# The last stage of a four-stage network on one core: bias by a one-row matmul, scale and shift on ScalarE, the row added behind, stores on SyncE

## The reference, cut to what matters

```python
for e in range(4):
    sl = slice(e * n, (e + 1) * n)
    m = d // 2 ** e
    out = attn_out[:, sl, :m] @ o_w[:m, :m].T + o_b[:m]
    outs.append(pad(out, d - m) + xn[:, sl, :])      # xn = layernorm of x
x = x + _layernorm(concatenate(outs))                # no weight, no bias, eps 1e-5
```

## Time and profile before

| | us |
|---|---|
| median of 3 runs | 5076.88 (5074.21 to 5078.27) |
| the profiled execution's own time | 5076.77 |
| its span | 5074.3 |
| last stage, first `AT` load issued to the end of the span | 4967.76 to 5074.3 |

### The profile page before, as it was taken

One profiled execution on the slowest core, in us unless ns is written; L12 is line 12 of the kernel. 1 busy time (PEld: TensorE's weight loads), 2 busy tenths in 40 slices (PEclk: granted clock), 3 DMA queues, 4 the chain that ended last, 5 costly groups with the idle time before them and its releaser, 6 DMA issues. The chain is left out here.

```text
span 5074.3 us, 90035 instructions
## 1 busy us (share of the span) xinstructions
PE 4656.5 (92%) x33915; PEld 2063.8 (41%) x33915; DVE 4191.1 (83%) x5487; ACT 3425.1 (67%) x6144; POOL 1333.4 (26%) x881
## 2 busy tenths in 40 slices
PE   6998776896999999999999999999998889999993
PEld 3333542562333333333333333333334445555532
DVE  6999640796999999999999999999993877777736
ACT  4878110232888888888888888888885426666663
POOL 2333210462000000000000000000001229999992
PEclk9999887995999999999999999999997769999996
DMA  5111569686333333333333333333313831322305
GB/s 183 58 54 42 187 241 390 201 271 136 49 49 49 49 49 52 53 53 53 49 49 49 49 49 49 54 54 54 49 20 125 297 101 43 82 61 73 79 5 169
DMA packets 383090, 479.51 MB, mean 94 GB/s; under 512 B 164544, under 2 KB 277984, under 8 KB 365760
## 3 DMA queue, kind: packets, MB, share of 16 engines
q1 hardware_dynamic: 369376, 455.41, 38.5%
q10 hardware_dynamic: 13280, 18.35, 1.1%
HBM read 315.71 MB, written 155.58 MB: 93 GB/s over the span
## 5 line engine op out<-in xcount | busy, mean ns | idle before, releaser
L792 DVE TENSOR_REDUCE at_NM<-at_MX 128x1 f32<-128x1024 f32 (+1 forms) x3008 | 3085.7, 1050 | 300.5 <-PE at_MX L614 272.2
L734 ACT ACTIVATE at_PB<-at_S 128x512 f32<-128x512 f32 x5056 | 2720.4, 597 | 587.6 <-PE at_S L643 465.6
L614 PE MATMUL at_MX<-at_KT,at_QT 48*128 48x512 f32 (+1 forms) x5056 | 1920.6, 455 | 58.6 <-DMA at_VS<-v 43.9
L643 PE MATMUL at_S<-at_QT,at_KT 50*128 50x512 f32 (+1 forms) x5056 | 1900.0, 441 | 6.1 <-ACT at_PB L734 5.8
L655 PE MATMUL at_AV<-at_PB,at_VS 128*32 128x256 f32 (+1 forms) x18304 | 1568.6, 414 | 16.6 <-ACT at_AVS L742 15.6
L643 PEld LDWEIGHTS at_S<-at_QT,at_KT 50*128 50x128 f32 (+1 forms) x5056 | 801.6, 187 | 879.0 <-ACT at_PB L734 773.6
L614 PEld LDWEIGHTS at_MX<-at_KT,at_QT 48*128 48x128 f32 (+1 forms) x5056 | 791.2, 190 | 310.2 <-DVE at_NM L792 215.6
L655 PEld LDWEIGHTS at_AV<-at_PB,at_VS 128*32 128x32 f32 x18304 | 363.3, 108 | 859.8 <-ACT at_PB L734 747.5
L548 POOL CAST at_NMR<-at_NMF 16x128 fp32r<-16x128 f32 x79 | 22.1, 279 | 1626.6 <-ACT at_NMF L747 1626.6
L575 POOL TENSOR_TENSOR at_SUM<-at_SUM,at_PB 128x2048 f32<-128x2048 f32 x90 | 415.1, 4612 | 10.9
L935 PE MATMUL wkv_PQ<-wkv_XT,wkv_WT 128*128 128x512 f32 x768 | 341.3, 601 | 50.5 <-DVE wkv_DL L1058 34.1
(11 more groups left out here) (213 smaller groups left out, 3492.6 us busy)
## 6 DMA issues: line engine op xcount, KB each, us to landing
at_QT<-qk SPq DMA_DIRECT2D x402, 128.0 KB, 4.9
moe_W<-in_w SPq DMA_DIRECT2D x48, 1024.0 KB, 11.8
at_KT<-qk SPq DMA_DIRECT2D x384, 128.0 KB, 6.6
qk<-r_HI SPq DMA_DIRECT2D x52, 512.0 KB, 4.7
qk<-r_LO SPq DMA_DIRECT2D x52, 512.0 KB, 5.3
at_VS<-v SPq DMA_DIRECT2D x96, 256.0 KB, 8.7
at_KT<-qk SPq DMA_DIRECT2D x96, 256.0 KB, 6.1
ycat<-wkv_Y SPq DMA_DIRECT2D x32, 512.0 KB, 2.6
```

The costliest lines, as they stand in the source:

```text
L614: ins = nc.tensor.matmul(MX[r][:, a, :], q_of(s)[h:h + NQ, b * P:(b + 1) * P], k_of(it, s, b * P // W)[h:h + NQ, (c + a) * W:(c + a + 1) * W],
L643: nc.tensor.matmul(SP_[item(it, s, "score", t)[1]][:, :], k_of(it, s, c)[h:h + NQ + 2, kb * P:(kb + 1) * P], q_of(s)[h:h + NQ + 2, c * W:( ...
L734: nc.scalar.activation(PB[:, t % NPB, :], SP_[r][:, :], ACT.Exp, scale=scale).then_inc(exp_done, 1)
L792: nc.vector.tensor_reduce(NM4[:, b, c:c + 1], MX[r][:, :, :].rearrange("p a n -> p (a n)"), AX_X, ALU.max, negate=True).then_inc(ring_got, 1)
```

## The change

- The bias `OB` is loaded as one row, and a row of ones `ONE` is set by POOL. For every 128 tokens PE adds one more matmul, `ONE` times `OB` with one row of contraction, into the same sum in `PA`. DVE's `PA += OB` and its semaphore are gone.
- ACT makes `XO = Z * RS + NB`; it waits for `NB` only. DVE's four operations `Z = Z * RS + X` are gone. In their place DVE makes `XO = XO + X` in one operation on 1024 elements, and counts `y_done` there. The shift `NB` has become `shift(g)`, and the add, now `result(g)`, runs one group later.
- SP issues the stores, each behind the `X` load of the same turn. `XO` has three buffers.
- POOL's power waits for `xo_done` instead of `nb_done`, since ACT now reads `RS`.

```diff
@@ SP
             for g in range(2, NGR):
                 load_a(g)
                 if g + 1 < NGR:
                     load_x(g + 1)
+                if g > 2:
+                    store(g - 3)       # waits y_done >= g - 2, then stores XO
+            for g in range(NGR - 3, NGR):
+                store(g)
...
@@ POOL
-                wait(pool, nb_done, g - 1)
+                wait(pool, xo_done, g - 1)
...
@@ PE
+            pe.wait_ge(ob_ld, 16)
+            pe.wait_ge(one_set, 1)
...
-                                               OW[0:k, c, 0:D >> e], start=(c == 0), stop=(c == len(cs) - 1))
+                                               OW[0:k, c, 0:D >> e], start=(c == 0), stop=False)
+                    ins = nc.tensor.matmul(PA[u][:, j, 0:D >> e], ONE[:, :], OB[:, 0:D >> e], start=False, stop=True)
...
@@ ACT
-                wait(act, y_done, g + 1)
                 wait(act, nb_done, g + 1)
-                wait(act, o_st[u], 16 * (g // 2))
+                wait(act, o_st[g % NO], 16 * (g // NO))
                 for j in range(J):
-                    ins = nc.scalar.activation(XO[u][:, j, :], Z[g % NZ][:, j, :], ACT.Identity, bias=NB[u][:, j:j + 1])
+                    ins = nc.scalar.activation(XO[g % NO][:, j, :], Z[g % NZ][:, j, :], ACT.Identity,
+                                               bias=NB[u][:, j:j + 1], scale=RS[u][:, j:j + 1])
                 ins.then_inc(xo_done, 1)
-                wait(act, xo_done, g + 1)
-                act.dma_start(group(tokens(out_d), g), XO[u][:, :, :]).then_inc(o_st[u], 16)
...
@@ DVE
-                nc.vector.tensor_tensor(PA[u][:, :, 0:mm], PA[u][:, :, 0:mm],
-                                        OB[:, 0:mm].unsqueeze(1).to_broadcast([P, J, mm]), ALU.add).then_inc(biased, 1)
-                wait(dve, biased, g + 1)
...
-                for j in range(J):
-                    ins = nc.vector.scalar_tensor_tensor(out=Z[g % NZ][:, j, :], in0=Z[g % NZ][:, j, :], scalar=RS[u][:, j:j + 1],
-                                                         in1=X[g % NX][:, j, :], op0=ALU.mult, op1=ALU.add)
-                ins.then_inc(y_done, 1)
+            def result(g):
+                wait(dve, xo_done, g + 1)
+                nc.vector.tensor_tensor(XO[g % NO][:, :, :], XO[g % NO][:, :, :], X[g % NX][:, :, :],
+                                        ALU.add).then_inc(y_done, 1)
...
                     stats(g + 1)
-                result(g)
+                shift(g)
+                if g > 0:
+                    result(g - 1)
+            result(NGR - 1)
```

More of the change, by code:

```diff
@@ L2220, in phase_final @@
     NGR = B * E4
-    NX, NZ = 4, 3
+    NX, NZ, NO = 4, 3, 3
     tag = "fin"
@@ L2227, in phase_final @@
         Z = [m.sb(f"Z{u}", [P, J, D]) for u in range(NZ)]
-        XO = [m.sb(f"XO{u}", [P, J, D]) for u in range(2)]
+        XO = [m.sb(f"XO{u}", [P, J, D]) for u in range(NO)]
         OW = m.sb("OW", [P, CC, D])
-        OB = m.sb("OB", [P, D])
+        OB = m.sb("OB", [1, D])
+        ONE = m.sb("ONE", [1, P])
         ST = [m.sb(f"ST{u}", [P, J, 6]) for u in range(2)]
@@ L2236, in phase_final @@
         PA = [m.ps(f"PA{u}", [P, J, D]) for u in range(2)]
-        ow_ld, ob_ld, half_set, a_done, biased, z_done, rest_done, stat, var, eps, rs, y_done, nb_done, xo_done = (
-            m.sem(n) for n in ("ow_ld", "ob_ld", "half_set", "a_done", "biased", "z_done", "rest_done", "stat", "var",
+        ow_ld, ob_ld, half_set, one_set, a_done, z_done, rest_done, stat, var, eps, rs, y_done, nb_done, xo_done = (
+            m.sem(n) for n in ("ow_ld", "ob_ld", "half_set", "one_set", "a_done", "z_done", "rest_done", "stat", "var",
                                "eps", "rs", "y_done", "nb_done", "xo_done"))
@@ L2241, in phase_final @@
         a_ld = [m.sem(f"a_ld{u}") for u in range(3)]
-        o_st = [m.sem(f"o_st{u}") for u in range(2)]
+        o_st = [m.sem(f"o_st{u}") for u in range(NO)]
         block = ctx.enter_context(nc.Block())
@@ L2265, in _ @@
             load_a(0)
-            sp.dma_start(OB[:, :], ob_d.partition_broadcast(P)).then_inc(ob_ld, 16)
+            sp.dma_start(OB[:, :], ob_d.partition_broadcast(1)).then_inc(ob_ld, 16)
             load_x(0)
@@ L2270, in _, with store @@
             load_x(2)
+            def store(g):
+                wait(sp, y_done, g + 1)
+                sp.dma_start(group(tokens(out_d), g), XO[g % NO][:, :, :]).then_inc(o_st[g % NO], 16)
             for g in range(2, NGR):
@@ L2274, in _ @@
                     load_x(g + 1)
+                if g > 2:
+                    store(g - 3)
+            for g in range(NGR - 3, NGR):
+                store(g)
+            for u in range(NO):
+                sp.wait_ge(o_st[u], 16 * len(range(u, NGR, NO)))
         @block.gpsimd
         def _(pool):
+            nc.gpsimd.memset(ONE[:, :], 1.0).then_inc(one_set, 1)
             nc.gpsimd.memset(nhalf[:, :], -0.5).then_inc(half_set, 1)
@@ L2318, in _ @@
                     rest(g + 2)
-                wait(act, y_done, g + 1)
                 wait(act, nb_done, g + 1)
-                wait(act, o_st[u], 16 * (g // 2))
+                wait(act, o_st[g % NO], 16 * (g // NO))
                 for j in range(J):
-                    ins = nc.scalar.activation(XO[u][:, j, :], Z[g % NZ][:, j, :], ACT.Identity, bias=NB[u][:, j:j + 1])
+                    ins = nc.scalar.activation(XO[g % NO][:, j, :], Z[g % NZ][:, j, :], ACT.Identity,
+                                               bias=NB[u][:, j:j + 1], scale=RS[u][:, j:j + 1])
                 ins.then_inc(xo_done, 1)
-                wait(act, xo_done, g + 1)
-                act.dma_start(group(tokens(out_d), g), XO[u][:, :, :]).then_inc(o_st[u], 16)
-            for u in range(2):
-                act.wait_ge(o_st[u], 8 * NGR)
         @block.vector
@@ L2357, in stats, with shift @@
                 ins.then_inc(var, 1)
-            def result(g):
+            def shift(g):
                 u = g % 2
@@ L2364, in result @@
                                                op0=ALU.mult, op1=ALU.mult).then_inc(nb_done, 1)
-                wait(dve, stat, g + 1)
-                for j in range(J):
-                    ins = nc.vector.scalar_tensor_tensor(out=Z[g % NZ][:, j, :], in0=Z[g % NZ][:, j, :], scalar=RS[u][:, j:j + 1],
-                                                         in1=X[g % NX][:, j, :], op0=ALU.mult, op1=ALU.add)
-                ins.then_inc(y_done, 1)
+            def result(g):
+                wait(dve, xo_done, g + 1)
+                nc.vector.tensor_tensor(XO[g % NO][:, :, :], XO[g % NO][:, :, :], X[g % NX][:, :, :],
+                                        ALU.add).then_inc(y_done, 1)
             add(0)
```

2 lines of the change are left out of this document (removed).

## The result

| kernel | median of its runs | lowest to highest | profiled execution (span) |
|---|---|---|---|
| before | 5075.56 us (4 runs) | 5074.21 to 5078.27 | 5076.77 (5074.3) |
| after | 5138.21 us (4 runs) | 5129.51 to 5140.94 | 5140.94 (5137.7) |

The ratio is 1.0116, 95% interval 1.0102 to 1.013: slower by 1.2%, 62.7 us between the medians. The forecast was 5100 us, with a range of 5085 to 5112. The direction is as forecast; the size is not, nearly three times what was said, and outside the range.

A forecast was written before the change was run, and what follows sets the result against it. The last stage was taken as bound by a ring of result, AT load, PE and DVE. Its first product, rounds of 32.1 us and tail added 22.8 us to 5076.9, rounded to 5100 us, range 5085 to 5112.

The forecast's parts named there:

- The ring: Last stage: AT waits for result(g-4), PE for AT, DVE for PE; a round takes 32.1 us against 23.5.
- DVE: Last stage: DVE spared 17.7 us, busy about 64 us; its turns take 4.7, 4.2, 3.9 and 3.8 us.
- The bias on PE: Quarter 0: eight added passes at the high clock cost 1.7 us, making PE's product 7.1 to about 7.8 us.
- rival 4: PE's clock stays at 1.2 GHz throughout: 24 passes take 10.2 us, total 5111 us; chance 10%.
- Quarter 2: PE's 16 passes, starting after long idling, take 3.8 us.
- The sum of it: Along the last stage, from first product through two rounds of 32.1 us to the tail: 22.8 us more.
- the tail: After group 12's product: last turns, AT(14) and PE, POOL, shift, XO and last add, 25.0 us to the last store.
- The landing: From X issue until AT lands: 6.4 us at quarter 0 with the store ahead in SP's queue, 5.5 at quarter 2.
- Rival 1: DVE's relief decides and the ring stays slack: faster, 5058 us; chance 3%.
- Rival 2: Bias matmuls cost next to nothing: round 28.5 us, total 5087 us; chance 12%.
- Rival 3: The store does not delay AT: 8 us less, total 5092 us; chance 15%.
- Rival 5: Something in the ring was read wrongly and it nets to nothing: 5077 us; chance 4%.

The follow-up runs named there:

- no_bias: After without the bias matmuls, so its output lacks the bias: stage 121.9 us, median 5089.07 us, 1.0024 of before.
- dve_early: bias_dve with every AT load issued one turn earlier, ahead of the X load that waits for a result: stage 104.0 us, 0.9983 of before.
- rows1_last: After with all eight one-row bias passes behind the sixteen others, a PSUM bank per 128 tokens: stage 135.0 us, 1.0053 of before.
- dve_act: bias_dve with the stores back on ACT's queue, behind the next group's XO: stage 127.8 us, 1.0060 of before.
- bias_dve: After with the bias added by DVE as before, not by PE: stage 131.5 us, 1.0040 of before.
- ahead_best: dve_act with five AT and X buffers, AT two turns ahead, 128-row bias matmuls ahead of PE's AT wait: stage 87.7 us, 0.9966 of before.
- rows1_pairs: After with one-row matmuls behind every two 128-token products, three height changes a group, a PSUM bank per 128 tokens: stage 142.6 us, 1.0068 of before.

## Why the prediction was wrong, point by point

**The ring: right.** It was read from the order of instructions and the waits, and each link is in the profile after. no_bias shows it without the matmuls, dve_early removes it by moving `AT` alone.

**DVE: right.** Its busy time in the stage was to be about 64 us and is 64.8; the turns 4.7 and 3.9 us, measured 4.7 (5065.73 to 5070.45) and 3.9 (5081.24 to 5085.16).

**The bias on PE: the step that failed.** "I take 8 at the high clock, 1.7 us, because they lengthen a run whose clock has risen by then" made a quarter 0 of 7.1 to 7.8 us; all four took 12.7. Two things stood in the place of this step. The clock did not rise: the passes are not behind the run but within it, two after every four, and rows1_last shows that the step would have held for passes behind it (1.99 us). And a change of height costs extra, which no term had: even rival 4's 10.2 us for 24 passes at the low clock was 2.5 short. So of the 4.9 us between 7.8 and 12.7 half is the clock and half the changes. The working bounded the price by a 32-row matmul of 0.45 us a pass, which was a uniform run; it said nothing on mixing. Quarter 2 was 5.0 us for 3.8.

**The sum of it.** The stage was forecast at 129.3 us (from before's 106.5 by the 22.8) and took 165.0. The 35.7 us between: first product 12.7 for 7.0, 5.7 more; DVE's wait for the products of groups 1 and 2 ahead of the result of group 0, 4.3; group 4's landing and product 7.2; two rounds of 40.1 for 32.1, 16.0; the tail 2.7; less 0.3 at the start. They add up to 35.6, up to rounding. Of these some 29 are PE's and some 5 are landings.

**The landing: 1.5 us low at quarter 0.** 6.4 forecast from the `X` issue, 7.9 measured (5045.11 to 5053.02); at quarter 2, 5.8 for 5.5. The 1.5 us for the store may be right in size, since even with the store on ACT's queue (dve_act) it was 6.7, 1.8 over before. But the reason given, that the store stands ahead in SP's own queue, shows in one round only (8.2 against 6.7 in the first of bias_dve and dve_act, then 7.0 and 6.8). Why `AT` took a median of 7.1 us from issue in after and 5.9 in bias_dve, with the same order of issues, isn't settled.

**The rivals.** Rival 1, DVE's relief decides, fell: DVE waited 97.4 us. It needed landing and PE together under 3.8 us, or, as ahead_best shows, `AT` early enough that they don't count. Rival 2 fell. Rival 3 fell: the landing did get longer, 7.9 us from the `X` issue and not 4.9, and dve_act bears out only that it matters little whose queue the store is in. Rival 4 had the right clock, and its time was still 27 us short. Rival 5 fell.

**The range.** It ended just above rival 4 and took each part by itself. The parts aren't additive: 25.0 and 22.8 us alone, 58.4 together. Where a ring has no slack, the upper bound of a term counts once in every round, and this bound was set too low.

**What is open.** Whether the many changes or the few rows keep the clock at 0.50 in the changed kernel is not separated: full passes first do raise it with one-row passes behind them, and one-row passes alone ahead don't. rows1_pairs, the same work with three changes in place of seven, had the high clock at three quarters 0 and not at the fourth (142.6 us of stage). The kernels with fewer changes also have a bank of `PA` for every 128 tokens, where after has two such steps in one bank; no run varies that alone.

## What to carry to other kernels

A small matmul of another height set between full ones was not small here: it stopped weight loads from running ahead, and it kept the clock low too; give it the same height, or put all of them behind or ahead of the run. When a count comes one turn later, look for what stands behind the instruction that waits for it: here an operand load that did not need the wait at all. Price an added operation by what runs beside it in the new order, and let its upper bound into the range once per round of the ring.

## What the runs showed of the hardware

**Rows of contraction.** One row and 32 rows cost the same (stage 165.0 and 164.0 us, 12.7 us for 24 passes in both), and both far more than 128 rows (141.4 us, 7.4 to 8.4). *The Trainium skill, TensorE: Matmul & The Clock Gate, LDWEIGHTS, has the time of a weight load depend on columns and not on rows; the loads of after agree, with 0.50 us for two of 128 rows (5025.56) and 0.50 for two of one row (5055.02). What costs where heights alternate is when a load starts.*

**A change of height.** Between 128 rows and one the next weight load starts 0.65 us after the last one ended, and six passes of 256 columns take 3.15 us in place of 2.5. Between 64 rows and one (64 columns) 16 passes took 5.0 us for twice 1.97, and between 32 rows and one 3.6 for twice 1.91.

**ACT's `XO` with a second operand per partition.** The groups by form of before and of after:

```profile
L2323 ACT ACTIVATE fin_XO<-fin_Z,fin_NB 128x256 f32<-128x256 f32 x64 | 27.3, 496 | 42.9 <-DVE fin_Z L2367 42.9
```

```profile
L2337 ACT ACTIVATE fin_XO<-fin_Z,fin_NB,fin_RS 128x256 f32<-128x256 f32 x64 | 33.1, 588 | 70.3 <-DVE fin_NB L2369 70.3
```

92 ns more for each. It was hidden, as the prediction had it, except in the tail.

**POOL beside DVE's add between SBUF tiles.** The same operation of after, alone and then beside such an add:

```profile
4999.19 0.23 POOL L2294 TENSOR_SCALAR fin_VE<-fin_MV 128x4 f32<-128x4 f32 x1 [3.83 <-DVE fin_MV L2362]
...
5127.80 1.22 DVE L2374 TENSOR_TENSOR fin_XO<-fin_XO,fin_X 128x1024 f32<-128x1024 f32 x1
...
5127.93 1.18 POOL L2294 TENSOR_SCALAR fin_VE<-fin_MV 128x4 f32<-128x4 f32 x1 [1.37 <-DVE fin_MV L2362]
```

Over the stage its mean went from 413 to 1061 ns. It stands nearly as long as DVE's add does, and `RS` comes that much later. In the ring DVE waited for PE anyway and it did not show; in the tail it is part of the 2.7 us.
